# A three-part edit of a four-layer kernel on one core: the low-rank stage unrolled with its weights first, the GRU's shift written by ScalarE with widened state products, and swapped waits in the first merged stage

## What is computed

```python
# layer 0, condition: a linear map with a low-rank part of its own for each sequence
y = einsum('bfi,oi->bfo', x, W) + fc_bias + (x @ v / 128) @ u.T / 16 + b
y = gelu(y)                                   # u = v = the 128x16 factors of the sequence
# layer 0, second condition: 128 steps, each needs the last one's h
gate = sigmoid(h @ Wh.T + z_t @ Wz.T + b);  h = tanh(h * (1 - alpha) + gate * z_t)
# layer 1, condition: an LSTM of 128 steps;  layer 2, second condition: a GRU of 128 steps
z = sigmoid(x_t @ W_z + h @ U_z + vz);  r = sigmoid(x_t @ W_r + h @ U_r + vr)
hh = tanh(x_t @ W + (r * h) @ U + vh);  h = (1 - z) * h + z * hh
```

## Time and profile before

| what | us |
|---|---|
| median of 3 runs | 4367.74 |
| profiled execution, its own time | 4368.54 |
| its span | 4366.7 |
| TensorE busy | 4132.9 (95%) |
| VectorE busy | 2432.7 (56%) |
| ScalarE busy | 1864.6 (43%) |
| low-rank stage | from 0 to 64.4 of the span |
| first merged stage, first to last Tanh of the LSTM | 422.5 to 774.7 |
| GRU, first to last Sigmoid of r | 2437.7 to 2713.7 |

### The profile page before, as it was taken

How to read it: one execution, slowest core, us unless ns; L and a number is a source line. 1 busy time by engine, 2 the same in 40 slices (tenths; PEclk the granted TensorE clock), 3 DMA queues, 4 the chain that set the end, 5 groups by cost and what they waited for, 6 DMA issues and landing times. The chain is left out here.

```text
span 4366.7 us, 117087 instructions
## 1 busy us (share of the span) xinstructions
PE 4132.9 (95%) x40848; PEld 2923.2 (67%) x40848; DVE 2432.7 (56%) x7468; ACT 1864.6 (43%) x4849; POOL 775.6 (18%) x3244
## 2 busy tenths in 40 slices
PE   6998999999999999999899999899999798989999
PEld 4555777777787455555555788787878455666666
DVE  5775665455554788887455444666666555531111
ACT  3433443333332466565233222566666453233333
POOL 1111221000000477666122000111111210000000
PEclk9999999999999999999899999999999998989999
DMA  1000000000000000000000000000000100000000
GB/s 57 0 0 26 1 0 1 27 0 0 0 0 0 11 2 2 1 1 1 36 0 0 4 0 0 2 3 3 3 3 3 56 0 1 0 1 6 3 5 8
DMA packets 4096, 29.02 MB, mean 7 GB/s; under 512 B 432, under 2 KB 944, under 8 KB 2352
## 3 DMA queue, kind: packets, MB, share of 16 engines
q1 hardware_dynamic: 3776, 24.97, 1.5%
HBM read 22.87 MB, written 2.10 MB: 6 GB/s over the span
## 5 line engine op out<-in xcount | busy, mean ns | idle before, releaser
L604 DVE TENSOR_REDUCE cells_row_max<-banks 128x4 f32<-128x512 f32 x384 | 238.3, 682 | 161.8 <-PE banks L397 161.8
L2361 ACT ACTIVATE experts_hidden<-banks,weights 128x512 f32<-128x512 f32 x256 | 175.8, 687 | 262.9 <-PE banks L2303 261.3
L761 PE MATMUL banks<-clock_fill 128*128 128x512 bf16 x900 | 275.8, 394 | 1.2 <-PEq L101 1.2
L2311 PEld LDWEIGHTS banks<-weights,experts_hidden 128*128 128x128 f32 x2048 | 238.6, 192 | 30.1 <-issue 30.1
L2381 DVE SCALAR_TENSOR_TENSOR experts_acc<-banks,experts_gate,experts_acc 128x128 f32<-128x128 f32 x224 | 63.1, 344 | 348.3 <-PE banks L2311 348.3
L2303 PE MATMUL banks<-act_a,weights 128*128 (+1 forms) x512 | 244.9, 609 | 11.8 <-PEq L101 11.1
L541 ACT ACTIVATE cells_probs<-banks 128x512 f32<-128x512 f32 x384 | 198.3, 603 | 98.4 <-PE banks L437 90.0
L2311 PE MATMUL banks<-weights,experts_hidden 128*128 128x128 f32 x2048 | 238.8, 274 | 0.0
L604 DVE TENSOR_REDUCE attn_row_max<-banks 128x4 f32<-128x512 f32 x256 | 158.8, 682 | 133.2 <-PE banks L397 133.2
L1582 ACT ACTIVATE wave_hidden_turned<-banks,weights 128x128 f32<-128x128 f32 x512 | 206.6, 460 | 38.4 <-PE banks L1526 36.2
L2579 ACT ACTIVATE lin_context_turned<-banks 128x256 f32<-128x256 f32 x128 | 49.1, 384 | 402.7 <-PE banks L2531 402.7
(11 more groups left out here) (552 smaller groups left out, 10101.1 us busy)
## 6 DMA issues: line engine op xcount, KB each, us to landing
weights<-in_p SPq DMA_DIRECT2D x1, 2894.5 KB, 16.9
weights<-in_p SPq DMA_DIRECT2D x1, 2894.0 KB, 9.5
weights<-in_p SPq DMA_DIRECT2D x2, 1396.0 KB, 7.6
x_res<-in_x SPq DMA_DIRECT2D x1, 2048.0 KB, 15.3
out_x<-x_res SPq DMA_DIRECT2D x8, 256.0 KB, 2.0
weights<-in_p SPq DMA_DIRECT2D x1, 1836.0 KB, 10.9
weights<-in_p SPq DMA_DIRECT2D x1, 1835.5 KB, 6.9
weights<-in_p SPq DMA_DIRECT2D x1, 1344.5 KB, 9.9
```

The source lines that it names most:

```text
L604: dve.tensor_reduce(mt[:, 4 * g:4 * g + 4], bank, AX_X, ALU.max).then_inc(s["max_ready"], 1)
L761: pe.matmul(core.ps[:, bank, :], core.fill[:, 0:P], core.fill[:, :], start=True, stop=True)
L2311: last = pe.matmul(ps[:, OUT + e % 2, t * P:(t + 1) * P], hs[:, e % 2 * DEPTH + f, t * P:(t + 1) * P], w("W2", (e * DEPTH + f) * P, P), st ...
L2361: act.activation(hs[:, e % 2 * DEPTH + f, :], ps[:, f % 2, :], ACT.Gelu, bias=w("b1", j, 1)).then_inc(s["h_ready"], 1)
```

## The change

1. **Low-rank stage.** The load of p0 is cut: the first 645 columns (W, biases, projections) with a semaphore of its own (`w`), then constants and x, then the two 1 MB bias tables, then p1. POOL's copies go. All loops are written out. TensorE makes all 32 Gram matrices when the factors are there, four to a bank in four banks; then come 28 zero products; then it waits for x and makes the 32 products. VectorE makes the weights four sequences at a time into `core.a`, and after all of them splits the bias in two halves of 1024 columns. ScalarE calls Gelu once at the start, then 32 times, then makes the third bf16 part.
2. **First merged stage.** `FILLS` is (1, 2, 1, 2). The leaky product writes four copies of its 32 columns. The two waits of L1134 change places.
3. **GRU.** ScalarE's Copy writes the shift into the bank (`set_shift`), and TensorE's identity product stays only for the first two groups. VectorE makes `less = (z - 1) * h` in one operation instead of two; the weights of `ahead` are negated once. The products with zc and with r*h write two copies of their columns for r and the candidate, and four for z and for both of `ahead`. Zero products: none in the first three steps of a group, two in the fourth before the candidate, none at the end of a step.

```diff
@@ low_rank_stage
         def _(sp):
+            first = WIDTH["p0"] - 32 * P
             sp.dma_start(core.b[0:16, :], dram["factors"]).then_inc(core.loaded["f"], 16)
-            load_pack(sp, core, dram, 0)
+            sp.dma_start(core.region[0][:, 0:first], dram["p0"][:, 0:first]).then_inc(core.loaded["w"], 16)
             sp.dma_start(core.ctile[:, :], dram["const"]).then_inc(core.loaded["const"], 16)
             sp.dma_start(core.x[:, :], dram["x"]).then_inc(core.loaded["x"], 16)
+            middle = first + 16 * P
+            for lo, hi in ((middle, WIDTH["p0"]), (first, middle)):
+                sp.dma_start(core.region[0][:, lo:hi], dram["p0"][:, lo:hi]).then_inc(core.loaded["p0"], 16)
             load_pack(sp, core, dram, 1)
...
         def _(pe):
+            pe.wait_ge(core.loaded["f"], 16)
+            for q in range(QUADS):
+                past(pe, s["weight_ready"], q - 3)
+                for j in range(4):
+                    factor = core.b[0:16, tok((4 * q + j) * P, P)]
+                    last = pe.matmul(ps[:, GRAM + q % 4, j * P:(j + 1) * P], factor, factor, start=True, stop=True)
+                last.then_inc(s["gram_done"], 1)
+            pe.wait_ge(core.filled, 1)
+            fill_clock(pe, core, FIRST_FILLS, Y + 3)
             pe.wait_ge(core.loaded["x"], 16)
+            for q in range(QUADS):
+                pe.wait_ge(s["weight_ready"], q + 1)
+                past(pe, s["gelu_done"], 4 * (q - 3))
+                for j in range(4):
+                    b = 4 * q + j
+                    last = pe.matmul(ps[:, Y + q % 4, j * P:(j + 1) * P], core.a[:, tok(b * P, P)],
+                                     core.x[:, tok(b * P, P)], start=True, stop=True)
+                last.then_inc(s["y_done"], 1)
...
         def _(act):
+            act.wait_ge(core.loaded["w"], 16)
+            act.activation(root[:, :], w("fc_bias"), ACT.Gelu).then_inc(s["root_ready"], 1)
+            act.wait_ge(s["shift_ready"], 1)
+            for b in range(NB):
+                act.wait_ge(s["y_done"], b // 4 + 1)
+                act.activation(core.a[:, tok(b * P, P)], ps[:, Y + b // 4 % 4, b % 4 * P:(b % 4 + 1) * P], ACT.Gelu,
+                               bias=shift[:, b:b + 1]).then_inc(s["gelu_done"], 1)
+            for h in range(HALVES):
+                act.wait_ge(s["left_ready"], h + 1)
+                act.activation(part(2, h), left[:, 1, h, :], ACT.Copy).then_inc(s["parts_ready"], 1)
...
@@ leaky_experts_lstm_stage
-    FILLS = (2, 3, 2, 3)
+    FILLS = (1, 2, 1, 2)
...
-                pe.matmul(ps[:, 2 + st.c // 4 % 2, lo:lo + NB].unsqueeze(1), w("WhT"), leaky_state(st), start=False,
+                out = ps[:, 2 + st.c // 4 % 2, :].rearrange("p (j t) -> p j t", j=4)
+                pe.matmul(out[:, :, lo:lo + NB], w("WhT"), leaky_state(st).broadcast_to([P, 4, NB]), start=False,
...
             def state(st):
+                dve.wait_ge(s["tc_ready"], st.s(1 - FIRST_LAG))
                 dve.wait_ge(s["gate_ready"], st.s(1 - FIRST_LAG))
-                dve.wait_ge(s["tc_ready"], st.s(1 - FIRST_LAG))
...
@@ gru_stage
             def step(t, k, g):
                 parity, rec = recurrent(k)
                 past(pe, zc_ready, t)
-                rec(R, "Ur", zc[:, :, :], True).then_inc(r_done, 1)
-                rec(Z, "Uz", zc[:, :, :], True).then_inc(z_done, 1)
-                more = not isinstance(t, int) or t < P - AHEAD
-                if k % AHEAD < 3 and more:
-                    pre(t + (AHEAD - k % AHEAD), 1 - parity, k % AHEAD)
-                fill_clock(pe, core, 1 if k % AHEAD < 3 else 3)
+                rec(R, w("Ur"), zc[:, :, :], True, 2).then_inc(r_done, 1)
+                rec(Z, w("Uz"), zc[:, :, :], True, 4).then_inc(z_done, 1)
+                which = k % AHEAD
+                if which < 3 and (not isinstance(t, int) or t < P - AHEAD):
+                    past(pe, shift_set, g * 3 + (which - 2))
+                    pre(t + (AHEAD - which), 1 - parity, which)
+                else:
+                    fill_clock(pe, core, 2)
                 pe.wait_ge(rh_ready, t + 1)
-                rec(CAND, "U", rh[:, :, :], True).then_inc(cand_done, 1)
+                rec(CAND, w("U"), rh[:, :, :], True, 2).then_inc(cand_done, 1)
                 if not isinstance(t, int) or t < P - 1:
                     ahead(t + 1, k + 1)
-                fill_clock(pe, core, 1)
...
+                if k % AHEAD == 3 and more:
+                    act.wait_ge(r_ready, t + 1)
+                    set_shift(0, bank)
+                if k % AHEAD == 0 and more and not (isinstance(t, int) and t == 0):
+                    act.wait_ge(z_ready, t)
+                    set_shift(1, 1 - bank)
+                if k % AHEAD == 1 and more and not (isinstance(t, int) and t == 1):
+                    act.wait_ge(cand_ready, t - 1)
+                    set_shift(2, 1 - bank)
                 act.wait_ge(cand_done, t + 1)
...
-                dve.tensor_tensor(zh[:, :, :], z[:, :, :], state(t), ALU.mult).then_inc(zh_ready, 1)
-                dve.wait_ge(zh_ready, t + 1)
-                dve.tensor_tensor(rest[:, :, :], state(t), zh[:, :, :], ALU.subtract).then_inc(rest_ready, 1)
+                dve.scalar_tensor_tensor(out=less[:, :, :], in0=z[:, :, :], scalar=1.0, in1=state(t),
+                                         op0=ALU.subtract, op1=ALU.mult).then_inc(less_ready, 1)
```

More of the change, by code:

```diff
@@ L167, in _ @@
         @block.tensor
         def _(pe):
-            pe.wait_ge(core.loaded["x"], 16)
[L171 to L183, removed]
@@ new lines, in _ @@
+            wait_pack(dve, core, 0)
+            whole = lambda h: w("relT", h * WIDE, WIDE)
+            for h in range(HALVES):
+                dve.tensor_copy(part(0, h), whole(h)).then_inc(s["split"], 1)
+            for h in range(HALVES):
+                dve.wait_ge(s["split"], h + 1)
+                dve.tensor_tensor(left[:, 0, h, :], whole(h), part(0, h), ALU.subtract).then_inc(s["split"], 1)
+            for h in range(HALVES):
+                dve.wait_ge(s["split"], HALVES + h + 1)
+                dve.tensor_copy(part(1, h), left[:, 0, h, :]).then_inc(s["split"], 1)
@@ L227, in _ @@
+            for h in range(HALVES):
+                dve.wait_ge(s["split"], 2 * HALVES + h + 1)
+                dve.tensor_tensor(left[:, 1, h, :], left[:, 0, h, :], part(1, h), ALU.subtract).then_inc(
+                    s["left_ready"], 1)
         @block.scalar
         def _(act):
-            act.wait_ge(shift_ready, 1)
-            with act.Fori(0, NB // 2) as i:
-                for p in range(2):
-                    b = i * 2 + p
-                    act.wait_ge(y_done, b + 1)
-                    act.activation(core.a[:, tok(b * P, P)], ps[:, 2 + p, 0:P], ACT.Gelu,
-                                   bias=shift[:, tok(b, 1)]).then_inc(gelu_done, 1)
+            act.wait_ge(core.loaded["w"], 16)
@@ L1895, in state, with run, group_bank, shifts @@
             return start_state[:, :, :] if isinstance(t, int) and t == 0 else positions(core.a, t - 1)
+        def run(eng, step):
+            for k in range(UNROLL_T):
+                step(k, k, k // AHEAD)
+            with eng.Fori(0, P // UNROLL_T - 2) as i:
+                for k in range(UNROLL_T):
+                    step(i * UNROLL_T + (UNROLL_T + k), k, i * 2 + (2 + k // AHEAD))
+            for k in range(UNROLL_T):
+                t = P - UNROLL_T + k
+                step(t, k, t // AHEAD)
+        def group_bank(which, parity):
+            bank = (R, Z, CAND)[which] + parity
+            return ps[:, bank, 0:AHEAD * NB].rearrange("p (t b) -> p t b", t=AHEAD)
+        def shifts(which):
+            return shift[:, which:which + 1, :].broadcast_to([P, AHEAD, NB])
         @block.sync
@@ L1955, in _, with set_shift, step @@
             fill_clock(pe, core, FIRST_FILLS)
+            pe.wait_ge(negated_ready, 2)
             ahead(0, 0)
-            time_loop(pe, step)
+            run(pe, step)
         @block.scalar
         def _(act):
-            def step(t, k):
+            def set_shift(which, parity):
+                act.activation(group_bank(which, parity), shifts(which), ACT.Copy).then_inc(shift_set, 1)
+            def step(t, k, g):
                 bank = k // AHEAD % 2
+                more = not isinstance(t, int) or t < P - UNROLL_T + 2
```

134 lines of the change are left out of this document (57 added, 77 removed).

## The result

The changed kernel takes 4296.13 us, the median of 4 runs (4295.51 to 4305.52), against 4368.05 us before: ratio 0.984, 95% interval 0.9823 to 0.9857. The forecast was 4298. The profiled execution is the slowest of the four, 4305.52 us with a span of 4303.7; the others have spans of 4293.7 to 4294.7. The trace therefore shows 63.0 us of the gain, the medians 71.9. The granted clock, averaged over the whole execution, was 0.974 in the profiled one and 0.976 in each of the others, so stage terms read from this trace carry a few microseconds of clock.

The account below looks back on a forecast made before the run. The step's period, not TensorE's busy time, was taken as the measure: in GRU partly TensorE's queue, in the low-rank stage first the wait for x. 4368.5 - 27.8 - 31.2 - 11.6 = 4298 us; 8-in-10 range 4283 to 4326.

Parts of the forecast that it names:

- the terms: Savings forecast for the three changed stages: low-rank 27.8 us, GRU 31.2, first merged stage 11.6.
- Low-rank, -27.8 forecast: Low-rank stage: the next stage would start at 37.3 us instead of 65.1; bounds 31 or 16 saved.
- I take the middle: Low-rank stage: next stage's start put at 37.3 us, between 34.2 and 40.4.
- Both cases: Low-rank stage: clock rises during Gram passes, next stage at 34.2 us; or only during zero products, at 40.4.
- 6.2 later: Low-rank stage: delay in us of everything if the clock rises only during the zero products.
- GRU, -31.2 forecast: GRU: 127 steps shortened from 2.172 to 1.92 us save 32.0; the start costs 0.8 more.
- The step of 1.92: GRU: new period in us, summed along the chain from the zc weights' load through r, r*h and candidate to the next.
- The rival of strided writing: GRU and merged stage: writing copies 128 columns apart is slow, GRU step 2.12, total 4325 us; chance 0.11.
- Merged stage, -11.6 forecast: First merged stage: swapped waits save 8.7 us, fewer zero products 4.1, leaky copies cost 1.2.
- its rival: First merged stage: swapping the waits does nothing, as the compiler orders them otherwise; total 4307 us; chance 0.11.
- 128 x 0.068 = 8.7: First merged stage: us saved by the swap, Tanh to state product falling from 0.20 to 0.13 in every step.
- The clock as rival on the slow side: GRU: runs at 1.2 GHz if copies don't count as work; steps about 2.8 us, total 4409; chance 0.05.

Follow-up runs that it names:

- e5_no_zeros: The changed kernel without the 28 zero products of the low-rank stage; median 4292.28 us, next stage starting at 33.2.
- e7_one_copy: The changed kernel with one copy instead of two in GRU's products of r and the candidate; median 4293.25 us.
- e8_no_copies: The changed kernel with one copy in all recurrent products of GRU; median 4388.45 us, ratio 1.0040 to the kernel before the change.
- e6_early_zeros: The changed kernel with 10 zero products before the wait for the factors instead of 28 after the Gram products; median 4288.15 us.
- e10_identity: The changed kernel with the identity product of the kernel before in place of ScalarE's Copy in GRU; median 4315.24 us.

## Why the prediction was right, point by point

- **Total.** 4298 forecast, 4296.13 measured. This is closer than the terms deserve: they measure -24.9, -29.1 and -10.5, 64.5 in all instead of 70.6. The medians gained 71.9. Every term was forecast too large, by 2.9, 2.1 and 1.1, and the hit within 2 us is luck: the medians gained 7 more than the terms. Runs and traces point to the clock in places that the change leaves alone. Kernels with one and the same last part need 1628.4 to 1637.1 us for it, those with the same LSTM 338.2 to 341.1, and the profiled execution of the changed kernel, from which the terms are read, was 9 us slower than its three others. Its mean granted clock of 0.974 against 0.976 fits that, since 0.002 of 4300 is 9 us; which of its stages made them isn't shown, since only one execution has a trace.
- **Low-rank, -27.8 forecast.** The failing step is "I take the middle". Both cases were worked out (34.2 and 40.4), and the trace shows the second within 0.1 us (40.28). That close it is luck as well: the "6.2 later" does not come out of the terms beside it (19.1 - 15.3 and 7.8 - 6 make 5.6), and the zero products took 9.1 instead of 7.8. The other parts hold: Gram 14.0 (13.7), first Gelu at 29.1 (22.6 + 6.2 = 28.8), last copies 1.1 each (1.04), split hidden behind the Gelus. VectorE's casts of 1024 columns took 0.65 rather than 1.2. The prediction did not ask whether the zero products were worth their place; e5_no_zeros shows that they were not.
- **GRU, -31.2 forecast, -29.1 measured.** The step of 1.92 held to the hundredth, though the eight terms listed for it add up to 1.90; the missing 0.02 are in the two loads, 0.06 instead of 0.05 after r x h and zc (2513.70 to 2513.76 above). The term that was missing is the loop head: 0.2 us in 14 steps, 2.8 us in all. Before, r x h had 0.3 us to spare behind TensorE's queue, and the turn of VectorE's loop was hidden by it; the change took that cover away, and I had not named what stood under it. The start, from the stage's first instruction to the first r, cost 0.3 instead of 0.8.
- **The copies.** At no cost in rate, 0.05 a step in latency, and necessary: e7_one_copy and e8_no_copies show the last two, the loads 0.11 apart the first. The rival of strided writing is refuted: passes that write 32-column runs 128 apart follow each other at 0.11, those that read x with a stride at 0.2. The Trainium skill, "PSUM — Partial Sum Buffer", Specifications, says that any non-contiguous access pattern slows matmuls significantly. These rows do not agree for this writing into PSUM, in runs of 32 columns.
- **Merged stage, -11.6 forecast.** -10.5 in the changed kernel (10.8 less 0.3 at its start) and -12.8 alone (13.6 less 0.8 at its start), of which 3.3 are the clock at the stage's end. The swap does what was said, 0.07 a step, and its rival falls. But 128 x 0.068 = 8.7 was booked on the wrong edit: one step in four gets nothing from it until a zero product goes. Only the sum by group was right, 4 x 0.068 + 0.11 = 0.38 against 0.41 measured. A head of a loop pass costs 0.15 here, too; on which engine, no run shows.
- **The clock as rival on the slow side.** It did not happen, but e8_no_copies shows that it was one edit away, at 2.63 us a step where 2.8 was estimated.

## What to carry to other kernels

When a stall in front of an operation is taken away, look what its engine does just before: a loop's branch and register work that were hidden can become part of the period, and a loop can be turned so that they fall where the engine idles. Work that only keeps the clock up has a price where it is on the path: put it where TensorE waits anyway, or widen products that run anyway, and test the kernel without it. Gains of a few microseconds are read from the stage, not from the total, since the total also moves by more than that in stages that no edit touched.

## What the runs showed of the hardware that was not expected

- Products with 16 rows of operands left the clock low for 14 us of unbroken work, and did not keep it when it had been raised (granted 0.99 from 5 to 10 us and 0.50 from 10 to 20 us in e6_early_zeros), while the y products of 128 rows raised it themselves (64 passes in 9.43 us in e5_no_zeros, where all at 0.21 would take 13.6).
- A single copy or four of the products of z and `ahead` made the difference between 2.63 us a step at 1.2 GHz and 1.87 to 1.92 at 2.4, though the engine was listed as busy in both: 326.00 of 326.00 us in the slow one.
- Of two waits written ahead of the state product on VectorE, the last one became an instruction of its own in both orders, and its place on the path was worth 0.07 us.
- At the high clock, identity products that read 32 columns of the shift, repeated four times, took 0.11 a pass (0.23 for two in e10_identity); products of the same shape that read x with a stride took 0.2, while the y products, which read x without one, took 0.11 (64 in 7.31 us).
